# A two-layer graph kernel: one of GpSimd's last gathers is replaced by single-row copies that ScalarE issues

## What is computed

```python
edge_input = concatenate([x[src], edge_attr_32])
messages   = gelu(edge_input @ mW1 + mb1) @ mW2 + mb2
gates      = sigmoid(gelu(edge_input @ gW1 + gb1) @ gW2 + gb2)
aggregated = segment_sum(messages * gates, dst)
update     = gelu(concatenate([x, aggregated]) @ uW1 + ub1) @ uW2 + ub2
x = layernorm(x + layernorm(x + update) * ln_g + ln_b)

Q, K, V = x @ Wq + bq, x @ Wk + bk, x @ Wv + bv      # 8 heads of 12
score = exp(clip(sum_head(K[src] * Q[dst] / sqrt(12) * (edge_attr_96 @ We + be)), -5, 5))
h     = segment_sum(V[src] * score, dst) / (segment_sum(score, dst) + 1e-6)
out   = layernorm(x + h)
```

## Time and profile before

| | before |
|---|---|
| median of 3 runs | 1237.32 us (1236.41 to 1237.65) |
| profiled execution, its time | 1236.37 us |
| profiled execution, its span (first to last instruction) | 1234.6 us |
| PE busy | 987.1 us, 80% of the span, 5213 instructions |
| DVE busy | 946.1 us, 77% |
| POOL busy | 931.4 us, 75%, 979 instructions |
| ACT busy | 688.0 us, 56% |
| mean granted TensorE clock | 0.942 |

### The profile page before, as it was taken

The page is one execution under the profiler, slowest core; times in us unless marked ns, Lnnn a source line. Parts: engine busy times, 40 slices in busy tenths (PEclk is TensorE's granted clock), DMA queues, the critical chain, the costliest instruction groups (busy, mean ns, idle before and its releaser), DMA issues. The chain is left out here.

```text
span 1234.6 us, 25653 instructions
## 1 busy us (share of the span) xinstructions
PE 987.1 (80%) x5213; PEld 627.4 (51%) x5213; DVE 946.1 (77%) x4242; ACT 688.0 (56%) x1522; POOL 931.4 (75%) x979
## 2 busy tenths in 40 slices
PE   5999999989999999999999505878887888888300
PEld 2555555548878878787877402433333333333100
DVE  3544444446999999999999963999999999999700
ACT  2555544432678788787878663555555555555300
POOL 6777777777777777777777777777777777777777
PEclk9999999999999999999999757999999999999755
DMA  7888888653567667677777445555555444434100
GB/s 170 235 231 229 226 227 217 139 156 108 187 210 229 212 222 225 213 226 217 229 209 232 143 159 131 146 143 133 132 144 140 128 128 135 133 115 131 37 31 30
DMA packets 174571, 206.35 MB, mean 167 GB/s; under 512 B 105195, under 2 KB 119596, under 8 KB 174505
## 3 DMA queue, kind: packets, MB, share of 16 engines
q1 hardware_dynamic: 140565, 159.21, 41.6%
q0 software_dynamic: 31200, 45.93, 15.9%
q10 hardware_dynamic: 2740, 0.60, 0.3%
HBM read 101.23 MB, written 77.58 MB: 145 GB/s over the span
## 5 line engine op out<-in xcount | busy, mean ns | idle before, releaser
L476 POOL DMA_INDIRECT out<-rows,put_at x196 | 190.6, 972 | 59.7 <-issue 35.0
L435 POOL DMA_INDIRECT agg_d<-rows,put_at x196 | 189.6, 967 | 59.8 <-issue 52.1
L426 POOL DMA_INDIRECT rows<-in_x,src_i x195 | 184.3, 945 | 62.1 <-issue 59.1
L454 POOL DMA_INDIRECT rows<-agg_d,dst_at x194 | 183.5, 946 | 60.5 <-issue 53.5
L469 POOL DMA_INDIRECT node_work<-agg_d,src_i x194 | 183.1, 944 | 59.1 <-issue 56.7
L719 ACT ACTIVATE node_work<-node_work,nshift,nscale 128x96 f32<-128x96 f32 x392 | 145.7, 453 | 81.8 <-DVE nshift L976 81.7
L754 ACT ACTIVATE rows<-yc,cshift,cscale 128x96 f32 (+1 forms) x196 | 75.5, 456 | 98.4 <-DVE cshift L1096 98.4
L853 DVE SCALAR_TENSOR_TENSOR ps<-hidden,ps 96x512 f32<-96x512 f32 x49 | 33.9, 691 | 125.5 <-ACT hidden L698 125.5
L487 PE MATMUL ps<-ident,x_in 128*96 128x128 f32 x588 | 81.7, 275 | 53.9 <-DMA ea<-in_edge_attr 52.7
L578 PE MATMUL ps<-uW2s,nT 97*128 97x96 f32 x784 | 99.7, 281 | 16.6 <-ACT nT L739 15.9
L940 DVE BATCH_NORM_STATS2 bn<-ps 128x6 f32<-128x96 f32 x392 | 100.2, 260 | 16.3 <-PE ps L578 16.1
(11 more groups left out here) (150 smaller groups left out, 2150.8 us busy)
## 6 DMA issues: line engine op xcount, KB each, us to landing
agg_d<-zeros SPq DMA_DIRECT2D x40, 480.0 KB
x_in<-in_x SPq DMA_DIRECT2D x49, 384.0 KB
node_work<-agg_d SPq DMA_DIRECT2D x49, 384.0 KB
agg_d<-node_work SPq DMA_DIRECT2D x49, 384.0 KB, 3.0
out<-node_work SPq DMA_DIRECT2D x49, 384.0 KB
mask<-cont_d SPq DMA_DIRECT2D x49, 208.0 KB
ein<-rows SPq DMA_DIRECT2D x49, 192.0 KB
mask<-cont_d SPq DMA_DIRECT2D x49, 192.0 KB
```

The costliest lines, as they stand in the source:

```text
L426: pool.indirect_dma_start(rows[:, g * EJ + j, :], None, x, rows_at(src_i, g, j)).then_inc(xs_gathered[g % 2][j], 16)
L435: pool.indirect_dma_start(agg_d, rows_at(put_at, g, j), rows[:, g * EJ + j, :], None).then_inc(agg_added[g % 2][j], 16)
L454: pool.indirect_dma_start(rows[:, g * EJ + j, :], None, x1_d, rows_at(dst_at, g, j)).then_inc(xd_gathered[g % 3][j], 16)
L476: pool.indirect_dma_start(out, rows_at(put_at, g, j), rows[:, g * EJ + j, :], None, bounds_check=N - 1, oob_is_err=False).then_inc(out_sca ...
```

## The change

GpSimd's pass 4 leaves out tile 193 (the second of group 48), so that it has one indirect DMA fewer. ScalarE fetches the 128 rows of `x1_d` by `src` for that tile: in each of the 40 loop steps of the attention stage it loads four row numbers from `tail_a` into registers and issues four copies of one row each, from HBM to HBM, into `tail_a_d`. SyncE, at group 48, waits for all 160 copies (the last 32 numbers are padding, zero) and loads tile 193 of `x1s` from `tail_a_d` by a transfer of its own, ahead of the one from `tail_rows`. ScalarE waits for the whole of `x1_d` before its attention stage. At the start there is one more memset on VectorE, one more load on ScalarE, and the counts of `pads_set` move by one.

```diff
+AFIRST, ASTEPS = 7, 40
+        tail_a_d = nc.dram_tensor("tail_a_d", [ASTEPS * 4, D], F32).ap()
+        tail_a = sb("tail_a", [1, ASTEPS * 4], I32)
...
-            sp.wait_ge(pads_set, 4)
+            sp.wait_ge(pads_set, 5)
...
-                for j in range(EJ - 2 if last else EJ):
+                for j in range(EJ - 3 if last else EJ):
                     sp.wait_ge(x1s_gathered[s][j], per_slot(g, s))
                 if last:
-                    sp.dma_start(x1s[:, g % XSLOTS, 0:EJ - 2, :], ahead[:, g % AHEAD, 0:EJ - 2, :]).then_inc(x1s_loaded[g % XSLOTS], 16)
+                    sp.dma_start(x1s[:, g % XSLOTS, 0:EJ - 3, :], ahead[:, g % AHEAD, 0:EJ - 3, :]).then_inc(x1s_loaded[g % XSLOTS], 16)
+                    sp.wait_ge(tail_a_fetched, 16 * 4 * ASTEPS)
+                    sp.dma_start(x1s[:, g % XSLOTS, EJ - 3, :], tail_a_d[0:P, :]).then_inc(x1s_loaded[g % XSLOTS], 16)
                     sp.dma_start(x1s[:, g % XSLOTS, EJ - 2:EJ, :], tail_rows[:, :, :]).then_inc(x1s_loaded[g % XSLOTS], 16)
...
-                for j in range(EJ - 2 if g == EFULL else EJ):
+                for j in range(EJ - 3 if g == EFULL else EJ):
                     pool.indirect_dma_start(ahead[:, g % AHEAD, j, :], None, x1_d, rows_at(src_i, g, j)).then_inc(x1s_gathered[g % 2][j], 16)
...
+            act.wait_ge(pads_set, 8)
+            act.dma_start(tail_a[0:1, 0:P], src[TFULL * P - 2 * P:TFULL * P - P].rearrange("(a p) -> a p", a=1)).then_inc(tail_a_loaded, 16)
...
                     act.activation(score[:, :], clip[:, :], ACT.Exp).then_inc(score_made, 1)
-
+                if inner:
+                    k = i * 4 - AFIRST * 4
+                    _, nodes = nc.values_load_multi_w_load_instructions(tail_a[0:1, bass.DynSlice(k, 4)], engines=[mybir.EngineType.Activation], min_val=0, max_val=N - 1,
+                                                                        skip_runtime_bounds_check_because="src holds rows of x")
+                    for n, node in enumerate(nodes):
+                        act.dma_start(tail_a_d[bass.DynSlice(k + n, 1), :], x1_d[bass.DynSlice(node, 1), :]).then_inc(tail_a_fetched, 16)
+
+            act.wait_ge(tail_a_loaded, 16)
+            for t in range(2):
+                act.wait_ge(x1_stored[t], slot_total(t))
             sweep(act, -1, EGROUPS + 3, 8, 4, attend_step, XSLOTS)
...
+            dve.memset(tail_a[:, P:], 0).then_inc(pads_set, 1)
```

More of the change, by code:

```diff
@@ L236, in build @@
         lnb_placed = sem("lnb_placed")
+        tail_a_loaded, tail_a_fetched = sem("tail_a_loaded"), sem("tail_a_fetched")
         tail_x_loaded, tail_x_fetched, tail_x_placed = sem("tail_x_loaded"), sem("tail_x_fetched"), sem("tail_x_placed")
@@ L635, in attend_step @@
                 if inner or i + 1 < EGROUPS:
-                    pe.wait_ge(x1s_loaded[(q + 1) % XSLOTS], per_slot4(i + 1, (q + 1) % XSLOTS) + (0 if inner or i + 1 < EFULL else 16))
+                    pe.wait_ge(x1s_loaded[(q + 1) % XSLOTS], per_slot4(i + 1, (q + 1) % XSLOTS) + (0 if inner or i + 1 < EFULL else 32))
                     pe.wait_ge(x1d_loaded[1 - s], per_slot(i + 1, 1 - s))
@@ L671, in _ @@
                 act.dma_start(to[:], row(of).broadcast_to([P, D])).then_inc(weights_loaded, 16)
-            act.wait_ge(pads_set, 7)
+            act.wait_ge(pads_set, 8)
             act.dma_start(Wvs[:, 0:D], Wv).then_inc(weights_loaded, 16)
             act.dma_start(bvs[0:D, :], column(bv)).then_inc(weights_loaded, 16)
+            act.wait_ge(pads_set, 8)
+            act.dma_start(tail_a[0:1, 0:P], src[TFULL * P - 2 * P:TFULL * P - P].rearrange("(a p) -> a p", a=1)).then_inc(tail_a_loaded, 16)
             act.wait_ge(edge_weights_loaded, EDGE_WEIGHTS)
@@ L828, in _ @@
             dve.tensor_scalar(need[:], pairs[:], 16, None, ALU.mult).then_inc(needs_made, 1)
-            dve.wait_ge(pads_set, 7)
+            dve.wait_ge(pads_set, 8)
             dve.wait_ge(edge_weights_loaded, EDGE_WEIGHTS)
```

## The result

| | before | after |
|---|---|---|
| median of 22 runs each, side by side | 1237.25 us (1236.05 to 1238.99) | 1235.59 us (1234.63 to 1236.96) |
| profiled execution: time, span | 1236.37, 1234.6 us | 1234.95, 1233.1 us |

The ratio is 0.9985, 95% interval 0.9979 to 0.9991: between 1.1 and 2.6 us less, 1.66 in the middle. The forecast was 1.25 less. It is inside what was called the same, and a little on the fast side of it. Each ratio here compares undisturbed executions alone, so it can differ a little from that of the two medians.

The account below looks back on a forecast made before the run. GpSimd's queue was taken to set the end: 1237.32 - 1.25 = 1236.1 us, with the attention stage's 44 + 4 = 48 us hidden under a cover of 56.9. The range for 8 in 10 was 1234.6 to 1256.

Parts of the forecast that it names:

- What bounds and what is removed: GpSimd's queue of 979 instructions sets the end; one gather less in pass 4 takes away 1.25 us.
- The lead: ScalarE's rows precede GpSimd's last pass by least at group 47: 58.1 us, 56.9 after the change.
- In order on ScalarE: In each loop step `kS` waits for the added load and issues, starting 4.58 us after the clip's end.
- The Trainium skill's rule: Rival on ScalarE: activations pass the issues, step stays near 8.27 us, time 1236.1 us; chance 0.10.
- The load, 0.58 by a line between one and eight numbers: ScalarE's load of four numbers per step: 0.58 us, between SyncE's 0.28 for one and 0.99 for eight.
- costs what it costs on GpSimd: Rival: ScalarE's register load takes 1.30 us for four numbers, GpSimd waits 20 us, time 1256; chance 0.27.
- the 0.80 of the prediction: Length of ScalarE's register load, in us, above which GpSimd starts to wait.
- The issue, 0.92 each: Each of ScalarE's four row copies per step costs 0.92 us, from one SyncE row; four are 3.70.
- Contention of two sequencers: Rival: SyncE's and ScalarE's issues delay each other, 16 us over 35 steps, time 1243 up to 1256; chance 0.15.
- The last group's stall: At group 48 SyncE's wait for ScalarE's last copies delays PE's operand: one stall of about 4 us.
- Faster: Case of gaining more than the one gather, which would take cheaper GpSimd instructions; chance 0.04.
- The margin was called thin: Cover allows 1.32 us growth per step, 1.10 used; an added block 0.22 us longer turns the case.

Follow-up runs that it names:

- e9: Against the kernel after: four numbers per step, all moved by one word in `tail_a`; 1968.83 us, ratio 1.0168, on a slow chip.

## Why the prediction was right, and where its sizes were not

The time was right because the mechanism was: one gather less on the queue that sets the end, and everything added stays under another engine's lead. But under the cover the time does not depend on the length of the added block, so the time does not confirm the sizes worked out for that block. Those were tested only by the trace, and most of them were too large.

- **What bounds and what is removed.** Right. One indirect DMA is 1.25 us by the rows, and its removal gave 1.66 (1.1 to 2.6), 1.45 for the gather alone and 2.57 for two.
- **The lead.** Right as the number that decides: of 58.1 us, 1.25 went with the gather and 20.4 with the slower stage, and 36.4 are left. The five- and six-row kernels spend it, and the time then rises by what is over it: within 3 us in the medians, within 5 in the profiled execution with five rows.
- **In order on ScalarE.** Right. `kS` waits for the issues in all 40 steps, seen in ScalarE's waits after, from 820 to 1200 us, and VectorE waits for `kS`:

```profile
ACT hidden L758 <- issue: 118.5, 40, 3.8
```

```profile
DVE hidden L1040 <- ACT hidden L758: 22.9, 40, 1.4
```

  The Trainium skill's rule ("Advanced Engine Details and Errata", "Sequencer Loop"), by which `kS` would have started beside the issues, is not what ScalarE does here: in the step shown `kS` starts 0.48 us after the last of them has ended.
- **The load, 0.58 by a line between one and eight numbers.** Mis-sized: 0.31. The straight line between SyncE's loads of one and of eight numbers does not hold, because on ScalarE the cost goes by fours and their place. (SyncE's own eights all start at multiples of eight words and still take from 0.72 to 1.24 us; that spread stays open.) The rival "costs what it costs on GpSimd" falls for this kernel, by 1.30 to 0.31; but with the numbers one word further on the load takes 0.92 (e9), past the 0.80 of the prediction. With the issues as short as they are, the lead should still hold; by my estimate it takes 0.61 x 40 = 24 us of 36, which was not run on the chip with 1237. Part of GpSimd's higher times may be the place of its numbers too; no run separates it.
- **The issue, 0.92 each.** Mis-sized: 0.527 + 0.25 = 0.77. SyncE's same form took 0.647, so a row of one queue was not good for another to better than 20%. Together, 0.27 + 4 x 0.15 = 0.87 us per step; the step came out 0.76 shorter than forecast, and these two are most of the 28 us by which the last rows come ahead of the 1216 forecast.
- **Contention of two sequencers.** Not on ScalarE, where the prediction priced it: the lock that the Trainium skill tells of ("Perfetto Trace Analysis", "DMA Instruction — HWDGE") does not lengthen its issues. These are the issues beside SyncE's tail rows, in the window 1005 to 1022 us, SyncE's own in that window, and ScalarE's behind the last of them, from 1142 to 1148:

```profile
L783 ACTq DMA_DIRECT2D tail_a_d<-agg_d x8: 527/528/528, 1006.9 to 1017.9; - x8
...
L368 SPq DMA_DIRECT2D tail_rows<-agg_d x16: 224/228/338, 1005.1 to 1016.8; - x16
...
L783 ACTq DMA_DIRECT2D tail_a_d<-agg_d x4: 527/527/527, 1144.7 to 1147.0; - x4
```

  The 338 is the one issue of SyncE there that starts at the same time as one of ScalarE's, 1007.63. SyncE lost 0.1 us by it, for which nobody waited.
- **The last group's stall.** 3.49 against 4, but by errors that offset each other. The copies were all there about 1.3 us after the last issue, not 3.0; against that, PE had to wait 1161.35 - 1157.56 = 3.8 us from SyncE's first issue and not 2.75, since the last transfer queued behind the held load released it; and it wanted its operand 5.3 us after the clip instead of 6.2. What was left out is the clock behind the stall, 2.8 us more. Under the lead it cost nothing.
- **Faster.** The 0.4 us over one gather lies within the interval. I do not explain it.

The margin was called thin, 0.22 us per step. It was 36.4 / 40 = 0.91. The step that would have shown this is the price of the issue, which stood on one row of another engine.

## What to carry to other kernels

Where one engine's queue of equal instructions sets the end, take the period of one for each that is removed: that was the gain here, to a few tenths of a us. Then price the work given to a helper against the lead at its smallest point, as growth per step times steps; within the lead it is free and past it each us counts. On a chip without the lead the copies cost 1.0%. Place numbers for a register load in whole, aligned fours: on ScalarE eight took 0.72 us where seven out of place took 1.72.

## What was not expected of the hardware

- ScalarE's register load: 0.31 us for four numbers at a multiple of four words and 0.92 for four moved by one; 0.54 and 1.13 for five; 0.72 for eight in place.
- A single-row copy is issued in 0.53 us from HBM to HBM and 0.23 us into one SBUF partition.
- A wait of 3.49 us of PE at the end of the stage cost 2.8 more behind it, since the work there started at a granted clock of 0.50 instead of 1.00 and the transposes went from 0.60 to 1.06 us. The kernel without that wait kept 1.00.
- On three of the chips the kernel before takes 1935 to 1957 us instead of 1237, with nearly the same time for each GpSimd instruction (944 to 972 ns for a gather), a mean granted clock of 0.77 instead of 0.94, and long pauses between instructions of all engines. The cause is open.
